# Mamba block on one core: GpSimd computes the step size and its product with the inputs, products with B in four buffers, GpSimd's hold removed

## The reference, cut to what matters

```python
dt = softplus(einsum('blr,cr->blc', dt_in, dw) + db)
A = -exp(Alog)
def step(h, inp):
    dt_t, B_t, C_t, u_t = inp
    dA = exp(dt_t[..., None] * A)
    h = dA * h + (dt_t * u_t)[..., None] * B_t[:, None, :]
    y = einsum('bcn,bn->bc', h, C_t)
    return (h, y)
```

## Time and profile before

| | |
|---|---|
| time, median of 3 runs | 2159.1 us |
| profiled execution, span | 2159.5 us |
| VectorE busy, whole span | 1645.7 us (76%) |
| GpSimd busy, whole span | 1011.2 us (47%) |
| steps of the Mamba block, first to last scan | 46.3 to 832.9 us |
| scan, 858 elements, mean | 1935 ns |
| weigh, 858 elements, mean | 1043 ns |
| product with B on GpSimd, 858 elements, mean | 2485 ns |

### The profile page before, as it was taken

How to read it: one execution, slowest core, us unless ns; L and a number is a source line. 1 busy time by engine, 2 the same in 40 slices (tenths; PEclk the granted TensorE clock), 3 DMA queues, 4 the chain that set the end, 5 groups by cost and what they waited for, 6 DMA issues and landing times. The chain is left out here.

```text
span 2159.5 us, 49411 instructions
## 1 busy us (share of the span) xinstructions
PE 1857.5 (86%) x19547; PEld 1357.8 (63%) x19547; DVE 1645.7 (76%) x2609; ACT 1298.3 (60%) x2660; POOL 1011.2 (47%) x775
## 2 busy tenths in 40 slices
PE   7888888889888867897878878889788699999999
PEld 4444444444443323444568877767676599999999
DVE  4999999999999996678465442346554589999897
ACT  5777777777776645114345444252456388888886
POOL 1777777777777773110017777300440033333333
PEclk9999999999999999899679999898899699999999
DMA  3544444444444442520038889501730411112000
GB/s 130 167 132 132 126 137 132 132 132 127 128 139 140 132 137 55 126 45 1 7 100 236 258 257 256 139 1 73 231 114 12 187 64 64 65 65 69 14 7 7
DMA packets 98037, 241.63 MB, mean 112 GB/s; under 512 B 15024, under 2 KB 48320, under 8 KB 95504
## 3 DMA queue, kind: packets, MB, share of 16 engines
q1 hardware_dynamic: 89120, 218.12, 32.7%
q0 software_dynamic: 7680, 15.74, 3.2%
q10 hardware_dynamic: 1008, 4.62, 0.6%
HBM read 226.25 MB, written 12.19 MB: 110 GB/s over the span
## 5 line engine op out<-in xcount | busy, mean ns | idle before, releaser
L1119 POOL TENSOR_TENSOR dBu<-du,Bs 128x858 f32<-128x858 f32 (+1 forms) x240 | 588.2, 2452 | 203.4 <-DVE hst L1046 94.6
L574 PE MATMUL py<-hst,ident 128*128 128x429 f32 (+1 forms) x960 | 416.7, 565 | 95.9 <-DVE hst L1056 95.1
L1046 DVE TENSOR_TENSOR_SCAN hst<-dA,dBu 128x858 f32<-128x858 f32 (+1 forms) x240 | 457.8, 1908 | 17.1 <-ACT dA L889 13.7
L889 ACT ACTIVATE dA<-dt,negA 128x416 f32<-128x416 f32 (+1 forms) x480 | 269.5, 596 | 177.2 <-DVE hst L1046 175.6
L574 PEld LDWEIGHTS py<-hst,ident 128*128 128x128 f32 x960 | 183.6, 202 | 292.3 <-DVE hst L1056 169.0
L3444 POOL TENSOR_TENSOR hm<-h,mw 128x264 f32<-128x264 f32 x128 | 89.7, 701 | 391.0 <-DVE h L3424 391.0
L1056 DVE TENSOR_TENSOR hst<-hst,Cs 128x858 f32<-128x858 f32 (+1 forms) x240 | 246.5, 1027 | 0.0
L3315 PE MATMUL pg<-hs,wh 128*128 128x66 f16 x6144 | 218.8, 194 | 4.8 <-issue 4.7
L3315 PE MATMUL pg<-xm,wi 128*128 128x66 f16 x6144 | 214.6, 195 | 6.8 <-issue 5.4
L3315 PEld LDWEIGHTS pg<-hs,wh 128*128 128x128 f16 x6144 | 204.8, 98 | 8.6 <-issue 5.1
L3315 PEld LDWEIGHTS pg<-xm,wi 128*128 128x128 f16 x6144 | 202.0, 98 | 11.3 <-issue 5.9
(11 more groups left out here) (568 smaller groups left out, 3458.8 us busy)
## 6 DMA issues: line engine op xcount, KB each, us to landing
wb<-sf_w SPq DMA_DIRECT2D x96, 514.0 KB, 4.9
Bs<-bc_rows SPq DMA_DIRECT2D x96, 429.0 KB, 4.6
Cs<-bc_rows SPq DMA_DIRECT2D x96, 429.0 KB, 3.5
mw<-route_weights SPq DMA_DIRECT2D x8, 2112.0 KB, 10.1
wb<-gf_w SPq DMA_DIRECT2D x24, 514.0 KB, 4.9
Bs<-bc_rows SPq DMA_DIRECT2D x24, 396.0 KB, 5.0
Cs<-bc_rows SPq DMA_DIRECT2D x24, 396.0 KB, 4.6
mb<-route_masks SPq DMA_DIRECT2D x8, 1088.0 KB, 5.8
```

What stands on the lines that cost most here:

```text
L574: return nc.tensor.matmul(out, weight, moving, **kw)
L889: last = a(o, by_seq(dt[:, j % 2, h, 0:n])[:, :, 1:S], ACT.Exp, scale=negA[:, l, h * DST + k:h * DST + k + 1])
L1046: v.tensor_tensor_scan(hst[:, g % HR, 0:2 * n], dA[:, g % 2, 0:2 * n], dBu[:, g % 2, 0:2 * n], 0.0, ALU.mult, ALU.add).then_inc(h_ready, 1)
L1119: g_.tensor_tensor(dBu[:, g % 2, 0:2 * n].rearrange("p (a n) -> p a n", a=2), du[:, j % 2, :, 0:n], Bs[:, q % NBS, k % BG, 0:n].unsqueeze( ...
```

## The change

It does four things. `dt` and `du` of item 0 stay on VectorE (`first_step`). Those of the 14 later items go to GpSimd: `dt` after the product of k = 11 (`step_size`, which waits for the mended logarithm, `patched`), `du` after that of k = 13 (`step_inputs`). The products with B get four buffers in place of two, and wait for the scan of step g-4. The hold at k = 10 goes.

```diff
+DR = 4
-        dBu = sb("dBu", [128, 2, 2 * SCW])
+        dBu = sb("dBu", [128, DR, 2 * SCW])
...
                 v.copy_predicated(ln[:, :, 0:n], small[:, :, 0:n], t).then_inc(patched, 1)
-                dve.wait_ge(patched, j + 1)
-                dve.wait_ge(d_read, 2 * j + 2)
-                v.tensor_tensor(dt[:, j % 2, :, 0:n], pos[:, :, 0:n], ln[:, :, 0:n], ALU.add).then_inc(dt_done, 1)
-                dve.wait_ge(dt_done, j + 1)
-                dve.wait_ge(u_gated, j + 1)
-                if j >= 2:
-                    dve.wait_ge(dBu_ready, DST * (j - 1))
-                v.tensor_tensor(du[:, j % 2, :, 0:n], dt[:, j % 2, :, 0:n], u[:, j % 2, :, 0:n], ALU.mult).then_inc(du_done, 1)
+                if j == 0:
+                    first_step()
...
+            def step_size(j):
+                l, at, n = item(j)
+                pool.wait_ge(patched, j + 1)
+                pool.wait_ge(d_read, 2 * j + 2)
+                g_.tensor_tensor(dt[:, j % 2, :, 0:n], pos[:, :, 0:n], ln[:, :, 0:n], ALU.add).then_inc(dt_done, 1)
+
+            def step_inputs(j):
+                l, at, n = item(j)
+                pool.wait_ge(dt_done, j + 1)
+                pool.wait_ge(u_gated, j + 1)
+                g_.tensor_tensor(du[:, j % 2, :, 0:n], dt[:, j % 2, :, 0:n], u[:, j % 2, :, 0:n], ALU.mult).then_inc(du_done, 1)
...
-                if k == 10:
-                    if j + 1 < NI:
-                        pool.wait_ge(du_done, j + 2)
-                    if j >= 2:
-                        pool.wait_ge(m_scaled, j - 1)
                 if g % BG == 0:
                     pool.wait_ge(b_loaded[q % NBS], 16 * (q // NBS + 1))
-                if g >= 2:
-                    pool.wait_ge(h_ready, g - 1)
-                g_.tensor_tensor(dBu[:, g % 2, 0:2 * n].rearrange("p (a n) -> p a n", a=2), du[:, j % 2, :, 0:n],
+                if g >= DR:
+                    pool.wait_ge(h_ready, g - DR + 1)
+                g_.tensor_tensor(dBu[:, g % DR, 0:2 * n].rearrange("p (a n) -> p a n", a=2), du[:, j % 2, :, 0:n],
                                  Bs[:, q % NBS, k % BG, 0:n].unsqueeze(1).broadcast_to([128, 2, n]), ALU.mult).then_inc(dBu_ready, 1)
+                if j + 1 < NI and k == 11:
+                    step_size(j + 1)
+                if j + 1 < NI and k == 13:
+                    step_inputs(j + 1)
```

More of the change, by code:

```diff
@@ L988, in soften, with first_step @@
                 v.copy_predicated(ln[:, :, 0:n], small[:, :, 0:n], t).then_inc(patched, 1)
-                dve.wait_ge(patched, j + 1)
-                dve.wait_ge(d_read, 2 * j + 2)
-                v.tensor_tensor(dt[:, j % 2, :, 0:n], pos[:, :, 0:n], ln[:, :, 0:n], ALU.add).then_inc(dt_done, 1)
-                dve.wait_ge(dt_done, j + 1)
-                dve.wait_ge(u_gated, j + 1)
-                if j >= 2:
-                    dve.wait_ge(dBu_ready, DST * (j - 1))
-                v.tensor_tensor(du[:, j % 2, :, 0:n], dt[:, j % 2, :, 0:n], u[:, j % 2, :, 0:n], ALU.mult).then_inc(du_done, 1)
+                if j == 0:
+                    first_step()
+            def first_step():
+                l, at, n = item(0)
+                dve.wait_ge(patched, 1)
+                dve.wait_ge(d_read, 2)
+                v.tensor_tensor(dt[:, 0, :, 0:n], pos[:, :, 0:n], ln[:, :, 0:n], ALU.add).then_inc(dt_done, 1)
+                dve.wait_ge(dt_done, 1)
+                dve.wait_ge(u_gated, 1)
+                v.tensor_tensor(du[:, 0, :, 0:n], dt[:, 0, :, 0:n], u[:, 0, :, 0:n], ALU.mult).then_inc(du_done, 1)
             def gate(j):
@@ L1045, in scan @@
                 dve.wait_ge(dA_ready, g + 1)
-                v.tensor_tensor_scan(hst[:, g % HR, 0:2 * n], dA[:, g % 2, 0:2 * n], dBu[:, g % 2, 0:2 * n], 0.0, ALU.mult,
+                v.tensor_tensor_scan(hst[:, g % HR, 0:2 * n], dA[:, g % 2, 0:2 * n], dBu[:, g % DR, 0:2 * n], 0.0, ALU.mult,
                                      ALU.add).then_inc(h_ready, 1)
```

## The result

The changed kernel takes 2169.47 us, the median of 20 runs, against 2160.77 us for the kernel before, also 20 runs. The ratio is 1.0045, 95% interval 1.0031 to 1.0059: slower by some 10 us, within the 1% that the prediction called no change, and on the side it forecast (2163 us, range 2133 to 2188).

The account below looks back on a forecast made before the run. VectorE's list was taken to bound the Mamba block. Operations moved off it -28.2, hits +36.5, the hold's hits -1.6, waits for dA -3.0: +3.7 us on 2159.5, so 2163 us, range 2133 to 2188.

Parts of the forecast that it names:

- VectorE is the bound, and what leaves its list is saved: Mamba block: VectorE's list sets the time; dt and du leaving it in 14 items takes off 28.2 us.
- A product of 1.71 us: GpSimd: a product alone, and so dt or du, takes 1.71 us, with bounds of 1.64 and 1.99.
- Two hits per item of 2.5 to 3.0 us, 36.5 in all: GpSimd products starting just ahead of weighs delay VectorE twice per item, giving back 36.5 us; chance of this forecast 0.53.
- the hold's hits: Weighs lengthened by products after the hold at k = 10; these go with the hold, -1.6 us.
- the bound of a rival: Third rival: operations take 1.99 us, a hit costs 1.8, maybe three per item; about 2200 us, chance 0.18.
- Hits at weighs 8 and 9: VectorE after step 8 of each item: long weighs of 2.0 to 2.6 us at steps 8 and 9.
- The replay: One item worked through: GpSimd free at 4.66, its next product 0.07 us ahead of weigh 8.
- the first rival: No hits: GpSimd's operations end later, weighs always go first, VectorE keeps 32.8 us; 2127 us, chance 0.17.
- The other signs: Items of 53 to 54 us, mean weigh some 1.19 us, GpSimd waiting 2 to 3 us for the mended logarithm.
- The second rival: One hit per item: 21 us back against 32.8 saved; 2147 us, chance 0.12.
- No scan waits for a product, ScalarE follows, loads of B are in time: Mamba block: the two extra GpSimd operations starve no scan, ScalarE keeps up, loads of B are priced at nothing.
- Waits covered by the hits: Waits for dA of some 0.25 us before the scan of step 12 vanish in the hits, -3.0 us.

Follow-up runs that it names:

- experiment 3: The changed kernel with two product buffers in place of four; ratio 1.0123 to the kernel before.
- experiment 1: The changed kernel with GpSimd's dt and du left out, one-column memsets in their place; 2181.81 against 2213.71 us for the kernel before, ratio 0.985.
- experiment 6: The kernel before plus, per item, one unused GpSimd product (ratio 1.0023), or in its place a short memset (1.0003) or a long one (1.0017).
- experiment 7: The changed kernel with every GpSimd operation released by a scan's end, in a place of its own; 2142.6 against 2159.99 us for the kernel before, ratio 0.9908.

## Why the prediction was right, step by step

- **VectorE is the bound, and what leaves its list is saved.** Right: 31.2 us without the two operations, 32.8 worked out. Per item the step itself saved a little more than its 2.05 us: m now starts 1.02 us after the mending (in the timeline of item 6: 403.79 to 404.81), where dt started 1.16 us after it, a wait of VectorE for its own result that I had not counted, 14 x 0.14 = 2 us.
- **A product of 1.71 us.** Right for about seven in ten products, which took 1.7 to 1.8 us net of the weigh that they waited for; the others took up to 2.0, as the upper bound had it. For dt and du it was too short: they take 2.0 us (experiment 3; in item 7 above dt took 1.94 after m). Why operations of one size differ by 0.3 us, no run tells.
- **Two hits per item of 2.5 to 3.0 us, 36.5 in all.** Right in mechanism and number, short in size: 41.7 us on weighs, with the 1.6 us of the hold's hits already taken off, so 43.3 us. Two things make the difference. At steps 8 to 12 of the 14 items the hits cost some 40.3 us, 3.8 more than forecast, because where an operation takes 2.0 us a hit costs 1.8. I had named this length as the bound of a rival and not put it into the forecast's sum. And in item 0, with four free buffers at once, GpSimd runs its first products back to back: 4.1 us at steps 0, 3, 4 and 15, beside the 3.0 us of that item's own two hits. I had priced the four buffers alone at nothing; steps 0 and 3 of item 0 are hit in experiment 1 too.
- **Hits at weighs 8 and 9.** Wrong in eleven of 14 items by the prediction's own sign. It holds in items 3, 8 and 13 alone, whose dt has 792 elements, takes 1.8 us and ends 0.05 us ahead of weigh 8 (item 3, above). In the others dt ends 0.08 us or more after the weigh has started (461.72 in item 7), so that one passed first, and the hits fell a step or more later, mostly on weighs 9 and 10. The replay had dt ready 0.07 us ahead because it gave dt 1.71 us. That 0.07 us decides which weigh is hit, as the first rival held; it does not decide whether one is. That rival counted on the dice falling well every time; GpSimd stayed two operations behind until two weighs had paid.
- **The other signs.** An item of 53 to 54 us: 53.1. The mean weigh: 1.23 us, not 1.19. GpSimd's wait for the mended logarithm: 4.0 us on average, not 2 to 3. Long weighs nowhere else: not so in item 0. (The second rival's sum gives 2147.7 us, 2148 rather than 2147.)
- **No scan waits for a product, ScalarE follows, loads of B are in time.** Right: 2.1 us once as before; waits for dA 8.6 us; one wait of 2.6 us of GpSimd for a load of B, in item 0.
- **Waits covered by the hits.** 5.1 us of waits for dA vanished where 3.0 were set. The 3 us at step 12 are gone as forecast; most of the rest is the wait at step 5 of item 0, which varies by itself. But 4.2 us of waits of the LSTM cell for ScalarE (1.7 to 5.9 us) came, which I had not foreseen; 3.5 of them stand at step 1. Their cause was not tried; the probe product of experiment 6 brought them too.

The terms as measured: -30.2 (the step) + 41.7 (weighs) + 1.6 (one m that was hit; the group went from 7.9 to 9.5 us; it is in the last item, where no mended logarithm holds GpSimd back) - 5.1 + 4.2 = +12.2 us, against +10.1 us from the first to the last scan; 2 us are not accounted for. The forecast of +3.7 us is as near as it is partly by luck: hits, m and LSTM waits came out 12.6 us dearer than in its sum, the step and the waits for dA 4.1 us cheaper.

## What to carry to other kernels

Work that is moved from VectorE to GpSimd, reads SBUF there and stands beside VectorE operations with two SBUF inputs costs first by where it starts: VectorE loses time where it is in flight when one of them wants to start. How long it lasts then sets the price (0.5 to 0.85 us for an operation of 1.0 us, 1.8 for one of 2.0). So count the places between those operations, and release every GpSimd operation by the event that opens its place. A wait that looks idle (the hold), or a buffer count that looks too small (two), may be what keeps two engines in step; loosening it cost 21 and 37 us here with no work added. And a hit is best put ahead of a place where the engine would wait anyway, as in experiment 7.

## What the runs showed of the hardware that was not expected

- The exclusion is settled by who asked first, also when both wait: a product that was kept back by a weigh went ahead of ser, and a weigh that waited for a product went ahead of the next product. A weigh or ser of 858 elements that was kept waiting ended 0.90 to 0.91 us after the product that it waited for (1.03 to 1.05 us alone).
- A memset on GpSimd (0.75 us) that ran into a weigh cost the weigh nothing; a product (1.02 us) from the same point cost 0.5 to 0.85 us.
- An operation of GpSimd that ended up to 0.1 us after a weigh had started (461.72 against 461.64) cost it nothing either.
- On GpSimd dt and du of 858 elements took 2.0 us each, products with B of the same size 1.7 to 2.0 us.
- The profile shows the lost time only as longer durations (weighs of 1.99 to 2.82 us), in no table of waits.
- The kernel before took 2159.99 to 2163.53 us in three sets of runs and 2213.71 us in a fourth, on another chip; in the four kernels profiled there the extra time lay outside the Mamba block. Only ratios can be compared between sets.
